# Dealing score units later and more evenly, and moving every second turned tile's copy to VectorE

## The chip, the cores and the metric

The kernel runs on one core of a Trainium2 chip. A core has TensorE (matmuls; PE in the profile, its weight loads PEld), VectorE (DVE), ScalarE (ACT), GpSimd (POOL) and SyncE (SP, which here only issues DMAs). The metric is the device time of one launch in microseconds, the median of the runs.

## The reference

Two transformer layers over x (4 batches, 512 tokens, 320 features), with a context of 1601 rows of 192 features per batch. Each layer is self attention, cross attention to the context and a gated feed forward, each behind a layer norm and with a residual:

```python
h1 = _ln(x, n1_g, n1_b)
x = _attn(h1, h1, q1, k1, v1, o1_w, o1_b, heads) + x          # 20 heads of 16
h2 = _ln(x, n2_g, n2_b)
x = _attn(h2, context, q2, k2, v2, o2_w, o2_b, heads) + x
h3 = _ln(x, n3_g, n3_b)
a, g = jnp.split(h3 @ ff_w1 + ff_b1, 2, axis=-1)
x = a * jax.nn.gelu(g, approximate=False) @ ff_w2 + ff_b2 + x
```

Attention is the exact softmax: the maximum of each row of scores is taken off before the exponential.

## The kernel before

**Groups, steps and beats.** A layer of a batch is a block; there are 8 blocks (i = 0 to 7). Attention is done in groups of 4 heads: 5 groups for each block's self attention (kind S, 4 tiles of 128 keys) and 5 for its cross attention (kind C, 13 tiles). One tile of keys of one group is a step; there are 680 steps. Ten phases (PHASES) interleave the cross attention of block c with the self attention of block c+2. Each step has four beats. At beats 0 and 2 TensorE makes scores of two heads each (`scores`, line 1303) into two banks `pr`, and ScalarE takes their exponentials (line 1020). At beat 3 TensorE multiplies the exponentials of the step before with the values (`weigh`, line 1320).

**Fills.** All other matmul work (projections, transposes, feed forward) is cut into fills, mostly one per odd beat, which share one bank `pf`. TensorE may begin a fill only when the one before it has been copied out (`fill_free`). The fills of this change are the transposes: `t1`, `t2` (layer norm output turned, 3 per block, copied with gain and bias into `hT` by ScalarE, line 964) and `tc` (context turned, 8 per block, copied into `cT` by ScalarE, lines 1007 and 1008; the fourth and eighth hold only 65 columns, with one column more copied by an instruction of its own). `v1`, `k2`, `q2`, `ff2` are projections.

**Units.** Before a group's scores can be made, the row maxima must be known. They come from units: a matmul pair into one of two banks `pd` (line 1287), and a maximum over its columns on VectorE (line 1111). An S group has 8 units of 2 x 512 columns, a C group 32 units of 2 x 400 (or 402) columns. When all are done VectorE forms the negated maxima (lines 1123 to 1135), and GpSimd issues a DMA that puts them into rows of the queries QS (`put_maxima`, line 913); the group's first scores wait for that (`max_in`). A unit needs its group's queries and keys in SBUF: SyncE stages them from DRAM scratch (`stage_group`, lines 781 and 786), at beats in STAGE_AT.

**The planner.** Which beat makes which units is worked out in plain Python ahead of the kernel. `beat_times` gives each beat a planned time AT, in its own microseconds. A group's units may be dealt from UNITS_FROM, which is AT at the staging beat plus STAGED_IN (6.0 for S, 8.0 for C), and should be dealt by UNITS_TO, 9.5 before the group's first step. At each even beat (in a step with one short fill: at beat 0 alone, with two places) the planner works out a rate, what is left over the time left, and a need, what is left over the places left, rounded up. The credit grows by rate x time, is at least the need, and is capped at the need or 2; whole credits are dealt as units, to the group of lowest number first:

```python
        _need = max(_need, -(-_sum * unit_places(_b) // _count))
    _credit = min(max(_credit + _rate * (_next - _now), _need), max(_need, MOST_UNITS))
    while _credit >= 1.0:
```

All engines run their lists of instructions in order of beats. At a beat VectorE does the work beside (norm statistics, residual adds, gates), then the reductions of that beat's units, then reciprocals. `set_key_rows` (lines 1044 to 1050, four memsets of KS) stands behind the work of the first beat (-1), ahead of the first units.

Of the kernel before, what the change touches and what calls it, by code (L numbers as in the profile page):

```python
# [12 lines left out]
P = 128  # L13
# [355 lines left out]


AT = beat_times()
STAGED_IN = {"S": 6.0, "C": 8.0}
LAST_UNIT_AHEAD, PUT_BEHIND, MOST_UNITS = 9.5, 0.5, 2

BEATS_AHEAD, LEAST_BEATS = 6, 8
# [22 lines left out]
for _q in GROUPS:  # L398
    for _part in range(-1, len(HALVES[_q.kind])):
        _stored = BEAT_OF[split_for(_q, _part)]  # L400
        _at = max(4 * read_until(_q, _part) if read_until(_q, _part) else FIRST_BEAT,
                  _stored + STORE + STAGE_BEHIND if _stored >= 0 else FIRST_BEAT)
        STAGE_AT.setdefault(_at, []).append((_q, _part))

        UNITS_FROM[_q.n, _part] = max(AT[_at] + STAGED_IN[_q.kind] if _at >= 0 else 0.0, UNITS_FROM.get((_q.n, -1), 0.0))
    UNITS_TO[_q.n] = AT[4 * _q.step0] - LAST_UNIT_AHEAD


# [11 lines left out]
for _b in range(0, BEATS, 2):  # L420
    if not unit_places(_b):
        continue
    _now = AT[_b]
    _next = AT[min(_b + 2 * unit_places(_b), BEATS - 1)]

    _rate, _need, _sum = 0.0, 0, 0
    for _n in sorted(n for n in _left if _left[n]):
        if units_now(_n, _now):
            _first_beat.setdefault(_n, _b)
        if _n not in _first_beat:  # L430
            continue
        _sum += units_now(_n, _now)
        _rate = max(_rate, _sum / max(UNITS_TO[_n] - _now, 0.5))
        _last = max(4 * GROUPS[_n].step0 - BEATS_AHEAD, min(_first_beat[_n] + LEAST_BEATS, 4 * GROUPS[_n].step0))
        _count = sum(unit_places(b) for b in range(_b, max(_last, _b + 2)))
        _need = max(_need, -(-_sum * unit_places(_b) // _count))
    _credit = min(max(_credit + _rate * (_next - _now), _need), max(_need, MOST_UNITS))
    while _credit >= 1.0:
        _n = next((n for n in sorted(_left) if _left[n] and units_now(n, _now)), None)
        if _n is None:  # L440
            break
        UNITS_AT[_b].append((_n, len(GROUPS[_n].units) - _left[_n]))
        _left[_n] -= 1
        _credit -= 1.0
        if not _left[_n]:
            assert _b < 4 * GROUPS[_n].step0
            PUT_AT.setdefault(min(beat_at(_now + PUT_BEHIND), 4 * GROUPS[_n].step0 - 1), []).append(GROUPS[_n])
# [33 lines left out]

def fills_at(beat):
    return sum(p[0] in STAGE for p in PLACES.get(beat, []))


LATE = {b for b in PLACES if 0 <= b < BEATS and b % 4 == 1 and fills_at(b) < 2 and not fills_at(b + 2)}
# [8 lines left out]
def blocks_kernel(nc, x, ctx_in, w, out):  # L495
    es = ExitStack()
    with es:
# [436 lines left out]
        def _(act):  # L934
# [8 lines left out]
            def beside(stage, i, f):  # L943
# [5 lines left out]
                if stage == "w" and f:  # L949
# [2 lines left out]
                    act.wait_ge(fill_ready, FILLS_BEFORE[stage, i, f])  # L952
                    hold(j)
                    copy(high_tile(j, P, KC * P), raw[:, :, :].rearrange("p k n -> p (k n)")).then_inc(raw_high, 1)
                if stage not in STAGE or stage in ("o1", "o2", "a", "ff2"):
                    return
                no = FILL[stage, i, f]
                pf, done = bank(no), free(no)
# [81 lines left out]
        def _(dve):  # L1040
            v = nc.vector
            dve.wait_ge(consts, CONSTS)
            v.tensor_copy(identr[:, :], DEN["S"][:, 0:P]).then_inc(identr_set, 1)
            def set_key_rows():

# [31 lines left out]
            def beside(stage, i, f):  # L1077
                l, b = i // B, i % B
                if stage in LN_STAGES:
                    measure(stage, i, f)  # L1080
                if stage == "n3" and i == N - 1:
                    if f:
                        normalise_last(f - 1)
                    if f == TT - 1:
                        normalise_last(f)
                if stage == "t3" and i == N - 1:
                    m = DC[f][1]
                    dve.wait_ge(h_high, KC * i + f + 1)
                    v.tensor_tensor(HS[0:m, 1, f, :], hT[0:m, f, :], HS[0:m, 0, f, :].bitcast(F32), ALU.subtract
                                    ).then_inc(h_low, 1)  # L1090
                if stage in ("o1", "o2", "ff2"):
                    s, no = {"o1": "n1", "o2": "n2", "ff2": "n3"}[stage], FILL[stage, i, f]
                    dve.wait_ge(bias_done, TT * LN0[s, i] + f + 1)
                    dve.wait_ge(fill_ready, no + 1)
                    v.tensor_tensor(X[:, b, f, :], bank(no)[:, 0:D], X[:, b, f, :], ALU.add).then_inc(free(no), 1)  # L1095
                if stage == "a":
                    no, side = FILL[stage, i, f], uT[:, f * T:(f + 1) * T]
                    if i < N - 1:
                        dve.wait_ge(gelu_done, FM * i + f + 1)
                    else:  # L1100
                        own, count = freed_through(FILL["g", i, f])[-1]
                        dve.wait_ge(own, count)
                    dve.wait_ge(fill_ready, no + 1)
                    v.scalar_tensor_tensor(side, bank(no)[:, :], b1col[:, l, 0, f:f + 1], side, ALU.add, ALU.mult
                                           ).then_inc(free(no), 1)
# [279 lines left out]
```

## Time and profile before

| | |
|---|---|
| median of 3 runs | 3407.88 us (3406.81 to 3412.51) |
| the profiled execution's own time | 3404.07 us |
| its span | 3402.3 us |
| PE, DVE, ACT, POOL busy | 3070.3 (90%), 2051.4 (60%), 1896.9 (56%), 729.4 us (21%) |
| units: reductions on VectorE | 1600, 1599.3 us in all |
| exponentials on ScalarE | 2720, 1478.4 us in all |
| mean granted TensorE clock | 0.96 |

The span is one execution from first to last instruction. A wait is put down to the instruction or DMA that ended it; "issue" stands where the profile shows no releaser. PEclk is the granted clock as a share of 2.4 GHz: 0.50 is the level of 1.2 GHz.

### The profile page before, as it was taken

The page shows a single profiled execution, that of the slowest core. Times are in us where ns is not written, and L with a number is a line of the kernel's source. Part 1 is how long each engine was busy: PE and PEld are TensorE (multiplying, and loading weights), DVE is VectorE, ACT ScalarE, POOL GpSimd, SP SyncE. Part 2 cuts the span into 40 slices and gives each one's busy share as a digit, 9 for nine tenths or more (in the row PEclk, how much of TensorE's full clock was granted, in tenths as well). Part 3 has the DMA queues.
Part 4 walks back from the last instruction along what each step waited for, and adds up shares of the span by engine and source line. Part 5 has one row for each costly group of instructions (what it writes and reads, how often), then busy time and mean ns, then how long its engine had stood idle before and what let it go on. Part 6 is the DMA issues. An engine that isn't in the chain of part 4 may idle for free.

```text
span 3402.3 us, 43794 instructions
## 1 busy us (share of the span) xinstructions
PE 3070.3 (90%) x16000; PEld 1412.6 (42%) x16000; DVE 2051.4 (60%) x2732; ACT 1896.9 (56%) x3646; POOL 729.4 (21%) x972
## 2 busy tenths in 40 slices
PE   4987888899999999999999899999998999998998
PEld 1332333334354343544345343453434543543445
DVE  5655655666656666656765576566665576666521
ACT  1643555656664566645665566745666466646631
POOL 2342221312302132022320223121231004002000
PEclk8997979999999999999999999999999999999999
DMA  6543334433433435433333334333243214322212
GB/s 158 154 111 93 112 85 120 126 110 84 129 105 83 129 81 148 108 90 117 98 117 88 118 94 136 100 96 104 64 125 101 79 40 137 96 51 49 73 38 78
DMA packets 208597, 342.27 MB, mean 101 GB/s; under 512 B 25464, under 2 KB 107776, under 8 KB 207104
## 3 DMA queue, kind: packets, MB, share of 16 engines
q1 hardware_dynamic: 203264, 338.09, 36.0%
q8 instruction: 128, 2.10, 0.3%
q0 software_dynamic: 5120, 1.39, 0.2%
q14 instruction: 85, 0.70, 0.1%
HBM read 202.29 MB, written 114.75 MB: 93 GB/s over the span
## 4 chain that ended last, share of the span: by engine, by line
PE 64%; DVE 14%; DMA 8%; ACT 6%; issue 4%; POOL 3%; SPq 2%; DVEq 0%; ACTq 0%; POOLq 0%
PE pr L1303 14%; PE po L1320 12%; DVE mx L1111 10%; PE pd L1287 7%; PE pf L1170 5%; PE pf L1223 5%; PE pf L1236 5%; ACT ET L1020 3%; PE pf L1193 3%; PE pf L1211 3%; DMA QS<-scr_q 3%; PE pf L1202 3%; DVE DEN L1119 2%; PE pf L1228 2%; DMA WS<-parts 1%
## 5 line engine op out<-in xcount | busy, mean ns | idle before, releaser
L1020 ACT ACTIVATE ET<-pr 128x512 f32<-128x512 f32 (+1 forms) x2720 | 1478.4, 597 | 1311.8 <-PE pr L1303 1300.0
L1111 DVE TENSOR_REDUCE mx<-pd 128x2 f32<-128x800 f32 (+2 forms) x1600 | 1599.3, 1031 | 941.9 <-PE pd L1287 939.3
L1303 PE MATMUL pr<-QS,KS 64*128 64x512 f32 (+1 forms) x2720 | 851.9, 503 | 70.6 <-ACT ET L1020 48.1
L1287 PE MATMUL pd<-KS,QS 64*128 64x400 f32 (+2 forms) x3200 | 633.7, 378 | 164.3 <-DVE mx L1111 102.1
L1320 PE MATMUL po<-ET,V 128*32 128x512 f32 (+2 forms) x5440 | 750.2, 625 | 0.5 <-ACT OU L1026 0.5
L1303 PEld LDWEIGHTS pr<-QS,KS 64*128 64x128 f32 (+1 forms) x2720 | 339.6, 185 | 907.4 <-ACT ET L1020 649.5
L1287 PEld LDWEIGHTS pd<-KS,QS 64*128 64x128 f32 x3200 | 373.2, 193 | 259.6 <-DVE mx L1111 167.2
L896 POOL TENSOR_TENSOR HS<-uT,HS 128x512 fp32r<-128x512 f32 (+4 forms) x168 | 190.1, 1132 | 613.0 <-ACT uT L984 612.7
L913 POOL DMA_DIRECT2D QS<-MT x160 | 94.1, 590 | 937.2 <-DVE MT L1135 934.5
L1223 PE MATMUL pf<-HS,WS 128*128 128x512 f32 x665 | 191.3, 418 | 13.1 <-issue 10.6
L1320 PEld LDWEIGHTS po<-ET,V 128*32 128x32 f32 (+2 forms) x5440 | 107.1, 108 | 208.2 <-issue 197.0
L1119 DVE RECIPROCAL DEN<-DEN 128x128 f32<-128x128 f32 (+1 forms) x192 | 168.9, 918 | 20.4 <-DMA OA<-OU 19.7
L1193 PE MATMUL pf<-cT,w_kv 96*128 96x400 f32 (+3 forms) x384 | 160.8, 542 | 9.3 <-ACT uT L984 5.3
L1236 PE MATMUL pf<-w_a,uT 128*128 128x320 f32 x560 | 158.1, 437 | 0.0
L921 POOL TENSOR_TENSOR OA<-OA,DEN 128x128 f32<-128x128 f32 (+1 forms) x192 | 84.9, 454 | 326.0 <-DVE DEN L1119 325.6
L1170 PE MATMUL pf<-hT,w_a 128*128 128x512 f32 (+1 forms) x288 | 139.7, 622 | 9.4 <-ACT uT L984 7.7
L1095 DVE TENSOR_TENSOR X<-pf,X 128x320 f32<-128x320 f32 x89 | 43.7, 491 | 171.2 <-PE pf L1236 119.4
L1223 PEld LDWEIGHTS pf<-HS,WS 128*128 128x128 f32 x665 | 115.7, 190 | 70.0 <-issue 34.1
L1202 PE MATMUL pf<-w_kv,cT 96*128 96x128 f32 (+3 forms) x832 | 139.6, 315 | 0.9 <-ACT V L988 0.5
L881 POOL TENSOR_SCALAR uT<-X,mv,rstd 128x320 f32<-128x320 f32 x92 | 133.9, 1456 | 9.7
L1211 PE MATMUL pf<-wo,OA 128*128 128x320 f32 x366 | 128.9, 473 | 4.7 <-POOL OA L921 3.5
L1202 PEld LDWEIGHTS pf<-w_kv,cT 96*128 96x128 f32 (+1 forms) x832 | 115.3, 189 | 29.2 <-issue 13.0
(81 smaller groups left out, 2053.2 us busy)
## 6 DMA issues: line engine op xcount, KB each, us to landing
WS<-parts SPq DMA_DIRECT2D x160, 320.0 KB, 3.0
QS<-scr_q SPq DMA_DIRECT2D x80, 512.0 KB, 5.8
scr_k<-HS SPq DMA_DIRECT2D x144, 200.0 KB
scr_q<-HS SPq DMA_DIRECT2D x96, 256.0 KB
KS<-scr_k SPq DMA_DIRECT2D x80, 300.8 KB, 5.2
KS<-scr_k SPq DMA_DIRECT2D x80, 300.0 KB, 6.1
KS<-scr_k SPq DMA_DIRECT2D x80, 192.0 KB, 4.8
scr_k<-HS SPq DMA_DIRECT2D x48, 256.0 KB
```

Of the source, the lines that this page charges most:

```text
L1020: activation(ET[0:q.rows[k], s % 2, 2 * pair + e, :], pr[e][0:q.rows[k], :], ACT.Exp).then_inc(score_free, 1)
L1111: v.reduce_max(mx[q.kind][:, t, 2 * p:2 * p + 2, c], pd[no % 2][:, :, 0:cols], AX_X).then_inc(unit_free, 1)
L1119: v.reciprocal(own, own).then_inc(inverted, 1)
L1170: ins = mm(pf[0:m, :], wsq[stage][:, k, r:r + m], hT[:, k, :], start=k == 0, stop=k == KC - 1)
L1193: ins = mm(pf[0:m, 0:cols], w_kv2[:, 0, k, r:r + m], cT[:, k, n0:n0 + cols], start=k == 0, stop=k == 1)
L1202: ins = mm(pf[0:m, to:to + (h1 - h0) * DH], cT[:, k, j * P:j * P + m], w_kv2[:, 1, k, h0 * DH:h1 * DH], start=k == 0, stop=k == 1)
L1211: ins = mm(pf[:, 0:D], OA[kind][0:m, k, t * P:(t + 1) * P], wo[0:m, which, k, :], start=k == 0, stop=k == KC - 1)
L1223: mm(pf[:, :], W[:, s, :], HS[:, 0, k, :], start=s == 0, stop=False)
L1236: ins = mm(pf[:, 0:D], uT[:, m * T + t * P:m * T + (t + 1) * P], wff2[:, m, :], start=m == 0, stop=m == FM - 1)
L1287: ins = mm(pd[no % 2][:, e, 0:cols], queries[:, t * P:(t + 1) * P], keys, start=True, stop=True)
L1303: mm(pr[e][0:m, :], keys, queries, start=True, stop=True).then_inc(score_ready, 1)
L1320: ins = mm(po[32 * h:32 * h + own.shape[1], :], own, ET[0:m, s % 2, h, :], start=k == 0, stop=k == q.kt - 1)
```

## The change

Four edits. First, units: S and C groups alike may be dealt units from 10.0 planned microseconds behind their staging (before: 6.0 and 8.0), and from 7.0 for the first ten groups, which run without a cross attention beside them (before: 6.0). Second, the need is kept as a fraction instead of being rounded up. Third, of the fills `t1`, `t2` and `tc` those with an odd f are copied out by VectorE: one of three for `t1` and `t2`, four of eight for `tc`. Fourth, since VectorE now reads the gains `gcol`, it waits at its start for the small loads (`small_in`), which ScalarE did already.

```diff
-STAGED_IN = {"S": 6.0, "C": 8.0}
+STAGED_IN, STAGED_ALONE = 10.0, 7.0
...
-        UNITS_FROM[_q.n, _part] = max(AT[_at] + STAGED_IN[_q.kind] if _at >= 0 else 0.0, UNITS_FROM.get((_q.n, -1), 0.0))
+        UNITS_FROM[_q.n, _part] = max(AT[_at] + (STAGED_ALONE if _q.n < 2 * G else STAGED_IN) if _at >= 0 else 0.0, UNITS_FROM.get((_q.n, -1), 0.0))
...
-    _rate, _need, _sum = 0.0, 0, 0
+    _rate, _need, _sum = 0.0, 0.0, 0
...
-        _need = max(_need, -(-_sum * unit_places(_b) // _count))
+        _need = max(_need, _sum * unit_places(_b) / _count)
...
-    while _credit >= 1.0:
+    while _credit >= 0.999:
...
+def taken_by_vector(stage, f):
+
+    return stage in ("t1", "t2", "tc") and f % 2 == 1
...
-                if stage not in STAGE or stage in ("o1", "o2", "a", "ff2"):
+                if stage not in STAGE or stage in ("o1", "o2", "a", "ff2") or taken_by_vector(stage, f):
                     return
...
             dve.wait_ge(consts, CONSTS)
+            dve.wait_ge(small_in, 16 * 2 * L)
...
+                if stage in ("t1", "t2", "tc") and taken_by_vector(stage, f):
+                    no = FILL[stage, i, f]
+                    dve.wait_ge(fill_ready, no + 1)
+                    if stage == "tc":
+                        c, (k0, k1) = f // len(TC_CHUNKS), TC_CHUNKS[f % len(TC_CHUNKS)]
+                        n0, cols = k0 * P, min(J, k1 * P) - k0 * P
+                        if k1 == JT:
+                            v.tensor_copy(cT[:, c, J:JP], bank(no)[0:CC, cols - 1:cols])
+                        v.tensor_copy(cT[:, c, n0:n0 + cols], bank(no)[0:CC, 0:cols]).then_inc(free(no), 1)
+                    else:
+                        s, m = int(stage[1]) - 1, DC[f][1]
+                        if LOWS_BEFORE[stage, i, f]:
+                            dve.wait_ge(h_low, LOWS_BEFORE[stage, i, f])
+                        v.tensor_scalar(hT[0:m, f, :], bank(no)[0:m, :], gcol[0:m, l, s, 0, f:f + 1],
+                                        gcol[0:m, l, s, 1, f:f + 1], ALU.mult, ALU.add).then_inc(free(no), 1)
```

## Rows read from the trace of the kernel before

**Rows 1.** The page's head and busy line: busy us, share of the span, instructions.

```profile
span 3402.3 us, 43794 instructions
PE 3070.3 (90%) x16000; PEld 1412.6 (42%) x16000; DVE 2051.4 (60%) x2732; ACT 1896.9 (56%) x3646; POOL 729.4 (21%) x972
```

**Rows 2.** Waits, whole span: engine, line waited for: us in total, times, longest.

```profile
PE pd L1287 <- DVE mx L1111: 102.1, 159, 2.7
...
PE pd L1287 <- issue: 53.9, 13, 16.6
...
PE pr L1303 <- ACT ET L1020: 48.1, 83, 6.3
...
PE pr L1303 <- DMA QS<-MT: 21.6, 7, 6.1
```

**Rows 3.** Groups of instructions by shape: S units' matmuls; busy, mean ns, idle before.

```profile
L1287 PE MATMUL pd<-KS,QS 64*128 64x512 f32 x640 | 140.5, 454 | 92.4 <-issue 53.9 <-DVE mx L1111 31.4 <-DMA QS<-scr_q 5.5
```

**Rows 4.** Timeline of PE, 1282 to 1295 us: start, us, what, [idle before].

```profile
1281.40 0.56 PE L1303 MATMUL pr<-QS,KS 64*128 64x512 f32 x2
...
1285.41 0.55 PE L1303 MATMUL pr<-QS,KS 64*128 64x512 f32 x2
1290.02 1.22 PE L1287 MATMUL pd<-KS,QS 64*128 64x512 f32 x4 [4.05 <-issue]
1291.17 3.03 PE L1193 MATMUL pf<-cT,w_kv 96*128 96x400 f32 x4
```

**Rows 5.** Windows of 8 us behind S groups' first units: window, us, busy times, PEclk, DMA.

```profile
343.90:351.90 8.00, 7.43 (x28) 3.57 (x28) 7.02 (x8) 2.25 (x5) 1.80 (x4) 0.67 0.14 39
...
1290.00:1298.00 8.00, 7.98 (x24) 3.15 (x26) 4.71 (x4) 1.88 (x4) 1.03 (x1) 0.50 0.51 165
...
2560.80:2568.80 8.00, 7.95 (x48) 3.85 (x48) 5.81 (x5) 2.43 (x5) 0.00 (x0) 0.79 0.36 98
```

**Rows 6.** The chain that ended last, 1275 to 1300 us: start, us, what.

```profile
1281.04 7.94 DMA QS<-scr_q
```

**Rows 7.** Timeline of PE, then of DVE, 1448 to 1465 us.

```profile
1453.05 0.49 PE L1287 MATMUL pd<-KS,QS 64*128 64x512 f32 x2 [0.58 <-DVE mx L1111]
...
1450.64 4.62 DVE L1111 TENSOR_REDUCE mx<-pd 128x2 f32<-128x1024 f32 x4
```

**Rows 8.** Waits of 186 to 328.7 us alone.

```profile
PE pd L1287 <- DVE mx L1111: 12.8, 22, 0.9
```

**Rows 9.** Groups by shape: reductions of C and S units, ScalarE's two copies.

```profile
L1111 DVE TENSOR_REDUCE mx<-pd 128x2 f32<-128x800 f32 x960 | 918.5, 985 | 537.1 <-PE pd L1287 536.3
L1111 DVE TENSOR_REDUCE mx<-pd 128x2 f32<-128x1024 f32 x320 | 373.8, 1216 | 203.3 <-PE pd L1287 202.1
...
L964 ACT ACTIVATE hT<-pf,gcol 128x512 f32<-128x512 f32 x47 | 36.8, 782 | 29.2 <-PE pf L1163 29.2
...
L1008 ACT COPY cT<-pf 96x512 f32<-96x512 f32 x48 | 28.0, 584 | 1.2 <-PE pf L1184 1.2
```

**Rows 10.** Timeline of DVE in a step with a turned context tile.

```profile
1243.55 1.89 DVE L1111 TENSOR_REDUCE mx<-pd 128x2 f32<-128x800 f32 x2 [1.15 <-PE pd L1287]
```

**Rows 11.** Start of the span: timeline; landing time of the loads of line 819.

```profile
3.95 0.43 SPq L819 DMA_DIRECT2D b1col<-ff_b_dram  x1
...
8.23 0.23 DVE L1043 CAST identr<-DEN 128x128 fp32r<-128x128 f32 x1 [8.23 <-POOL V L867]
...
12.35 6.25 DVE L1047 MEMSET KS<- 16x7432 f32 x1 [1.48 <-issue]
...
22.70 0.78 ACT L964 ACTIVATE hT<-pf,gcol 128x512 f32<-128x512 f32 x1 [1.21 <-PE pf L1163]
...
60.56 1.22 PE L1287 MATMUL pd<-KS,QS 64*128 64x512 f32 x4 [16.59 <-issue]
...
DMA to landing us min/median/max: 5.9/6.1/6.2
```

**Rows 12.** Timeline of PE, 2463 to 2476 us: a group's first scores.

```profile
2473.84 0.80 PE L1303 MATMUL pr<-QS,KS 64*128 64x512 f32 x2 [3.93 <-DMA QS<-MT]
```

## The prediction

> **What bounds the kernel now.** I read the page's head first: TensorE is busy for 3070.3 of 3402.3 us, VectorE for 60% and ScalarE for 56% [rows 1]. So the time is TensorE's: its work, plus what it idles, 332 us, plus what it loses while its clock is low. Next the list of waits, to see what ends TensorE's idle time. The largest entry is units: 102.1 us in 159 waits for a reduction that has not yet emptied a bank, and 53.9 us in 13 waits with no releaser named [rows 2]. The groups by shape say which units those 13 are: all are S units of 512 columns, which have 5.5 us more put down to the DMA of the queries [rows 3]. One of the 13 is the first unit of the kernel, 16.59 us [rows 11]. That leaves 53.9 - 16.6 = 37.3 us in 12 waits, and 5.5 us: 42.8 us of idle time in which TensorE stands at the first unit of an S group.
>
> The timeline shows one: scores at 1285.41, then nothing until 1290.02 [rows 4]. The chain gives the releaser that the wait does not: the DMA of that group's queries, issued at 1281.04, 7.94 us long [rows 6]. So the unit stands in TensorE's list before its data can be there; with "issue" the reader is to see a DMA. No C group's first unit waits: the shapes of 400 and 402 columns have nothing but reductions before them.
>
> Then the windows. Behind the wait TensorE is busy for 7.98 of 8 us, but at a granted clock of 0.50, the level of 1.2 GHz [rows 5]; a `k2` fill of four matmuls takes 3.03 us there [rows 4]. I took such a window behind the first unit of 13 S groups that had waited. Their clocks run from 0.50 to 1.00, and 8 x (1 - clock) adds up to 25.8 us (first, worst and last are in [rows 5]). Each long wait is paid for nearly twice.
>
> The waits for reductions are of another kind. Two S units in each of two successive even beats give VectorE four reductions, 4.62 us in a row, while TensorE goes through the short half of a step in less than half of that; the fourth unit waits 0.58 us [rows 7]. Such a burst comes out of rounding up: with 31 units left for 28 places the need is 2, not 1.1, so the planner deals two per beat until it is ahead, then one, and later none.
>
> **The change part by part.** The sum is made against the profiled execution, 3404.07 us, of which 1.8 us lie outside the span; the median is 3.8 us above it, which I add at the end.
>
> *S groups from 10.0 instead of 6.0.* For the group of the example the planner's times are: staged at 979.5, first unit at 987.1. From 989.5 on, the first even beat is the one at 990.9, two even beats (one step) later. TensorE takes 4.0 us for a step here (1281.40 to 1285.41, [rows 4]), and the wait was 4.05 us, so even this one ends about when the keys land. Other waits are 2 to 3 us and go; two early ones, of 7.65 and 4.61 us, may leave a remnant. Meanwhile C units are at hand to fill the beats. I take 4 us as left: **-39 us** (between -30 and -42.8). S maxima are not pressed: this group's first step is planned at 1028.4, 49 planned us behind its staging. With the long waits goes the low clock behind them, nine tenths of 25.8: **-23 us** (between -13 and -26).
>
> *C groups from 10.0 instead of 8.0.* There is no wait to remove. It costs places: each C group begins one even beat later, so that more units share the rest. The price is inside the next term.
>
> *Fractional needs.* Of the 102.1 us, 12.8 lie between 186 and 329 us [rows 8], where 40 units must pass in ten even beats, three to six per beat or pair of them; rounding does not matter there, and the C group starts a beat later: nothing gained. Of the other 89.3 us the runs of double S units and the doubles of C units go, since the rate then deals by planned time: two in the long halves of steps, one in the short ones. What stays are waits behind a group's maxima (some 1.5 us of small VectorE work), and the stretch of `t2` and `tc` steps. I worked the planner through there: 31 units for 25 places from its first S unit on, two places per step; the credit is capped at the need of 2.5, two are dealt, the need creeps up to 3, and the last four steps get three units each. VectorE then has 3 x 0.985 us [rows 9] plus a copy of some 0.7 us, in a step that lasts 3.04 us with two units (1.89 busy, 1.15 idle, [rows 10]) and a little more with three. I take 44% of the 89.3 us as removed, since I can follow the bursts away and not these: **-39 us** (between a fifth, -17, and two thirds, -61).
>
> *The last units come later.* Rounding up had units dealt ahead of their due time; now the last goes out one even beat later in some C groups. Behind it are the maxima, GpSimd's DMA and the first scores. One such wait exists: 3.93 us at 2473.84, where the transfer landed late [rows 12]; there are only seven in all, 21.6 us [rows 2], so most groups have room for one beat. **+8 us**, one more of that kind with its low clock (between 0 and +40).
>
> *Copies moved to VectorE.* Of 48, 32 have 512 columns: 16 from `hT`'s line, 0.782 us on ScalarE, and 16 from `cT`'s, 0.584 us [rows 9]. Nothing in the trace is such a copy on VectorE. The two reductions from PSUM give a slope: (1216 - 985) / 224 = 1.03 ns per column and 160 ns fixed, so 512 columns take 0.69 us, an estimate. With the 16 small pairs (65 columns and one, by the same line 0.23 + 0.16 us) that is 28.5 us more on VectorE. In a step with a context tile VectorE waits 1.15 us for its next unit [rows 10], so the copy fits where two units are dealt. The cover is gone where three are: +1 us taken, and all 28.5 us as the upper bound. VectorE's order puts nothing new in front of anybody: the fill is ahead of the next units on TensorE as well. On ScalarE the gain is bounded by TensorE's waits for exponentials in these steps, 0.1 to 0.5 us each within the 48.1 us of [rows 2]: **-3 us** (0 to -7).
>
> The Trainium skill speaks against this part: "VectorE: DVE Perf Modes", in its section on the TRN2 errata, has a PSUM source cost 120 cycles plus the columns at 0.96 GHz on VectorE, 172 plus the columns at 1.2 GHz on ScalarE. By that the copy would be an estimated 0.66 us on VectorE against 0.57 us on ScalarE, so the move makes the work itself longer; 28.5 us would become some 27. By the same formula the reduction of 1024 columns is 1.19 us, and the trace has 1.216 us.
>
> *The start.* VectorE begins at 8.23 us; the last small load is issued at 3.95 and takes at most 6.2 us, so it begins by 10.2 us [rows 11], and the first norm behind it. **+1.6 us** (0 to +1.9). Also the copy of `t1`'s second tile now stands before the four memsets of KS, the first of which began at 12.35 us; four of 6.25 us with three gaps of about 1.5 us take 29.5 us. That tile's copy began on ScalarE at 22.70 us [rows 11]; with 1.6 us of delay, 0.7 us of copy and 1.5 us of gap the memsets run from about 26.5 to 56 us. The first unit starts at 60.56 [rows 11], 4 us later, so this is hidden; without that cover each microsecond would count in full.
>
> The sum: -39 - 23 - 39 + 8 + 1 - 3 + 1.6 = -93.4; 3404.1 - 93.4 = 3310.7, and with 3.8 us to the median 3314 us.
>
> **The rivals.**
> *Only the DMA part holds.* The bursts form again, against the due times instead of ahead of them, and the copies sit in VectorE's full steps. For it: the 10.0 for C groups gives up places, and the hand-worked stretch ends in steps of three. Against: VectorE has 40% idle. Then -62 + 1.6 + 8 + 14 (half of the copies' time) = -38, 3369 us.
> *Slower: late maxima.* If the last units slip by two even beats, first scores wait as at 2473.84: 3.9 us, and about 4 us more of low clock behind it, 8 us per group. It decides from twelve groups on (93 / 8); in half of the 40 C groups it would be +160 us, 3474 us. For it: needs no longer force units forward. Against: UNITS_TO still stands 9.5 planned us ahead and the rate grows without bound as it nears, so that two beats are hard to lose.
> *No change.* The S transfer is released by the scores of an earlier step; should it be late for the queue and not for its issue, the units would wait at their new place. Then -15 for clock and bursts and +15 for the copies: 3408 us. Against: the queries of the example had landed at 1289 us [rows 6], whenever the unit is dealt.
> *More than forecast.* All of the 42.8, 25.8 and 89.3 us go, and 3 us of ScalarE, at no cost: 3247 us.
>
> **How the numbers follow.** The forecast gets 0.58, with its own range of 3280 to 3345; only the DMA part 0.24; late maxima 0.06; no change 0.05; more than forecast 0.07. The range goes from 3272, which takes about half of the last case, to 3375, just past the second: all but about 0.15 is inside. Faster by over 0.2% (what a measurement of this kernel can tell): 0.58 + 0.24 + 0.07 and 0.01 of no change, 0.90. Within 0.2%: 0.03. Slower: 0.06 and 0.01, 0.07.
>
> **What would show it.** In the waits, the 12 of TensorE for units without a releaser are down to two or three, and PEclk stays at 1.00 behind S groups' first units. The wait of `pd` for `mx` falls from 102.1 to about 60 us, and what is left stands in steps with three units. VectorE shows 32 copies of 0.6 to 0.75 us. QS<-MT grows by less than 10 us. The prediction is wrong if QS<-MT is ended by dozens of waits, if the keys' landing moves with the units, or if the first unit starts more than 2 us later than 60.56.

## The result and the profile after

| | before | after |
|---|---|---|
| median of 5 runs each, us | 3406.81 (3400.98 to 3412.51) | 3369.36 (3357.46 to 3381.6) |
| ratio, 95% interval | | 0.9896 (0.9865 to 0.9927) |
| profiled execution, us | 3404.07 | 3375.84 |
| its span; mean granted clock | 3402.3; 0.960 | 3374.0; 0.955 |

The change makes the kernel 1.04% faster, 37 us, where 93 were forecast. The time is inside the range (3272 to 3375), but by its upper end, where the rival "only the DMA part holds" had put it (3369 us).

The page's head of the kernel after, to hold against [rows 1]:

```profile
span 3374.0 us, 43804 instructions
PE 3074.7 (91%) x16000; PEld 1422.6 (42%) x16000; DVE 2072.7 (61%) x2796; ACT 1877.2 (56%) x3582; POOL 729.1 (22%) x972
```

The span of the profiled execution is 28.3 us shorter (the medians are 37.5 apart; the profiled execution of after lies 6.5 us above its median): TensorE idles 32.7 us less (332.0 to 299.3) and is busy 4.4 us more, for the same 16000 matmuls. I had forecast that busy time would fall, by the 23 us of low clock.

Waits of TensorE after, whole span (engine, line waited for, us in total, times, longest), against [rows 2]:

```profile
PE pd L1308 <- DVE mx L1132: 89.9, 135, 2.2
PE pr L1324 <- DMA QS<-MT: 51.2, 15, 6.8
PE pr L1324 <- ACT ET L1025: 44.7, 76, 4.9
...
PE pd L1308 <- DMA KS<-scr_k: 13.2, 1, 13.2
...
PE pd L1308 <- issue: 3.8, 1, 3.8
```

Units without their data: 59.4 us are now 17.0, of which 13.2 are the kernel's first unit. Units behind reductions: 102.1 to 89.9. First scores behind the maxima's DMA: 21.6 in 7 waits to 51.2 in 15. The last takes back 29.6 us of idle time; what that was worth in time is asked in the fourth series.

Groups by shape (busy, mean ns, idle before), S units' matmuls against [rows 3], then VectorE's new copies:

```profile
L1308 PE MATMUL pd<-KS,QS 64*128 64x512 f32 x640 | 137.4, 429 | 38.3 <-DVE mx L1132 21.1 <-DMA KS<-scr_k 13.2 <-issue 3.8
...
L1110 DVE TENSOR_SCALAR hT<-pf,gcol 128x512 f32<-128x512 f32 x16 | 12.9, 805 | 12.0 <-PE pf L1184 11.8
L1105 DVE COPY cT<-pf 96x512 f32<-96x512 f32 x16 | 10.8, 672 | 8.8 <-PE pf L1205 8.8
L1105 DVE COPY cT<-pf 96x65 f32<-96x65 f32 x16 | 3.4, 212 | 0.0
```

Windows of 8 us after (busy times, granted clock, DMA share, GB/s). The first begins with the late first scores of a C group, the second with the first unit of the S group that [rows 4, 5] show waiting:

```profile
878.30:886.30 8.00, 7.98 (x26) 3.32 (x26) 3.57 (x4) 3.10 (x7) 0.82 (x1) 0.50 0.75 191
1285.30:1293.30 8.00, 7.66 (x42) 2.99 (x41) 3.69 (x4) 5.53 (x12) 2.06 (x2) 1.00 0.42 117
```

Behind that S unit the clock is at 2.4 GHz where it was at 1.2. The level of 1.2 GHz now stands behind a wait of another kind.

The start after, timeline of VectorE and TensorE, against [rows 11]:

```profile
10.22 0.23 DVE L1049 CAST identr<-DEN 128x128 fp32r<-128x128 f32 x1 [10.22 <-DMA b1col<-ff_b_dram]
...
24.70 0.81 DVE L1110 TENSOR_SCALAR hT<-pf,gcol 128x512 f32<-128x512 f32 x1 [11.85 <-PE pf L1184]
...
50.55 6.25 DVE L1056 MEMSET KS<- 2x7432 f32 x1 [1.60 <-issue]
...
59.52 1.22 PE L1308 MATMUL pd<-KS,QS 64*128 64x512 f32 x4 [13.20 <-DMA KS<-scr_k]
```

The first unit is a microsecond earlier than before, not later.

### The profile page after: what moved, and what is told of

Its sections match the earlier page's. It is cut to its first block, busy times and chain, and to the rows that moved or that the text cites. A ratio compares the mean times of both kernels' runs of the same rounds, so it can differ in the third digit from the quotient of the medians.

```text
span 3374.0 us, 43804 instructions
## 1 busy us (share of the span) xinstructions
PE 3074.7 (91%) x16000; PEld 1422.6 (42%) x16000; DVE 2072.7 (61%) x2796; ACT 1877.2 (56%) x3582; POOL 729.1 (22%) x972
## 4 chain that ended last, share of the span: by engine, by line
PE 67%; DVE 13%; DMA 6%; ACT 6%; POOL 4%; issue 3%; SPq 2%; DVEq 0%; ACTq 0%; POOLq 0%
PE pr L1324 15%; PE po L1341 14%; DVE mx L1132 8%; PE pd L1308 7%; PE pf L1191 5%; PE pf L1244 5%; PE pf L1257 4%; PE pf L1214 4%; PE pf L1232 3%; ACT ET L1025 3%; PE pf L1223 3%; DVE DEN L1140 3%; DMA QS<-MT 2%; PE pf L1249 2%; DMA WS<-parts 1%
## 5 line engine op out<-in xcount | busy, mean ns | idle before, releaser
L1324 PE MATMUL pr<-QS,KS 64*128 64x512 f32 (+1 forms) x2720 | 860.9, 506 | 96.6 <-DMA QS<-MT 51.2
L1308 PE MATMUL pd<-KS,QS 64*128 64x400 f32 (+2 forms) x3200 | 620.3, 376 | 107.3 <-DVE mx L1132 89.9
```

The source lines that it names most:

```text
L1308: ins = mm(pd[no % 2][:, e, 0:cols], queries[:, t * P:(t + 1) * P], keys, start=True, stop=True)
L1324: mm(pr[e][0:m, :], keys, queries, start=True, stop=True).then_inc(score_ready, 1)
```

## The experiments

There are fifteen, in four series; each kernel's ratio is to the kernel before, run beside it on the same chip. A "step of three" below is one of the steps that have both of their places for units at beat 0 (at most one short fill beside them) and are dealt three units or more there. They are counted in the planner's lists, which it makes before anything runs: 46 in the kernel before, 47 in the kernel after.

| kernel | us | ratio (95%) | pd for a reduction | QS<-MT | low clock |
|---|---|---|---|---|---|
| before | 3401 to 3407 | 1 | 102.1 | 21.6 | 273 |
| after | 3369.36 | 0.9896 (0.9865-0.9927) | 89.9 | 51.2 | 300 |
| staging alone | 3427.28 | 1.0068 (1.0051-1.0086) | 143.7 | 21.5 | 257 |
| fractions alone | 3412.67 | 1.0023 (1.0012-1.0033) | 96.3 | 56.1 | 340 |
| copies alone | 3405.76 | 0.9992 (0.9976-1.0008) | 108.9 | 19.1 | 273 |
| all but copies | 3369.16 | 0.9897 (0.9881-0.9914) | 87.5 | 61.5 | 287 |
| after, C 8.0 | 3361.5 | 0.9884 (0.9863-0.9905) | 90.7 | 50.2 | 267 |
| staging of S alone | 3384.41 | 0.9945 (0.9924-0.9966) | 119.5 | 21.1 | 246 |
| after, 10 beats ahead | 3396.35 | 0.998 (0.9967-0.9993) | 122.5 | 20.7 | 269 |
| after, due 14 ahead | 3390.46 | 0.9953 (0.9935-0.9972) | 109.1 | 27.7 | 313 |
| after, halved reductions | 3269.11 | 0.961 (0.9583-0.9637) | 31.6 | 46.5 | 202 |
| before, halved reductions | 3290.98 | 0.9666 (0.9639-0.9693) | 33.2 | 17.4 | 212 |
| after, C 7.0 | 3352.59 | 0.9854 (0.983-0.9877) | 79.1 | 44.2 | 273 |
| after, C 7.0, MOST 2.5 | 3344.36 | 0.983 (0.9805-0.9854) | 80.5 | 38.8 | 263 |
| after, maxima put first | 3352.01 | 0.985 (0.9827-0.9874) | 91.4 | 16.4 | 253 |
| the last two together | 3338.47 | 0.9803 (0.9778-0.9828) | 74.5 | 14.5 | 245 |
| before, maxima put first | 3389.48 | 0.9954 (0.9937-0.9971) | 102.4 | 10.0 | 236 |

The last three columns are of each profiled execution, in us: two entries of the chain of waits, and the time in which the records show a granted clock under full.

### First series: the parts, one by one

**Staging alone.** The new times with the needs rounded up as before, and ScalarE's copies.

```diff
-STAGED_IN = {"S": 6.0, "C": 8.0}
+STAGED_IN, STAGED_ALONE = {"S": 10.0, "C": 10.0}, 7.0
...
```

> The kernel before with the staging times alone (10.0, and 7.0 for the first ten groups); needs are still rounded up and ScalarE copies all tiles. Theory A (fractions cost): the 42.8 us of waits at S groups' first units go and part of the low clock behind them, the last units stay where they were (12 even-and-odd beats ahead for 29 of 40 C groups), so QS<-MT stays near its 22 us and the time falls by 45 to 65 us, below the changed kernel. Theory B (the 10.0 of C groups costs): late maxima show up here already, QS<-MT near 50 us, and the time falls by 35 us or less.

It is 0.68% slower, and the theory by which the later times alone bring most of the gain falls. The S units' waits go (20.0 us named "issue" are left, 15.7 of them the first unit), but the waits for reductions rise by 41.6 us: rounded needs pack the units that begin later into what places are left (the planner's steps of three rise from 46 to 61). The waits of the kernel "staging alone":

```profile
PE pd L1287 <- DVE mx L1111: 143.7, 212, 3.0
...
PE pr L1303 <- DMA QS<-MT: 21.5, 6, 6.2
PE pd L1287 <- issue: 20.0, 4, 15.7
```

**Fractions alone.**

```diff
-    _rate, _need, _sum = 0.0, 0, 0
+    _rate, _need, _sum = 0.0, 0.0, 0
...
-        _need = max(_need, -(-_sum * unit_places(_b) // _count))
+        _need = max(_need, _sum * unit_places(_b) / _count)
...
-    while _credit >= 1.0:
+    while _credit >= 0.999:
```

> The kernel before with fractional needs alone. Theory A: the last unit of 15 of the 40 C groups moves from 12 or 10 beats to 8 beats ahead of the first scores, QS<-MT grows from 22 to about 50 us with low clock behind it, the waits for reductions fall by at most 15 us, and the time rises by 10 to 30 us. Theory B: fractions are worth the 15 us of waits that they remove, QS<-MT stays near 22 us, and the time falls by 10 to 20 us. My forecast had it at -31 us.

Slower as well, by 0.23%: 5.8 us less behind reductions, but 34.5 us more behind the maxima's DMA, and 66 us more at a low clock.

**Copies alone**, with VectorE's wait for the small loads.

```diff
+                if stage in ("t1", "t2", "tc") and taken_by_vector(stage, f):
+                    ...
+                    v.tensor_scalar(hT[0:m, f, :], bank(no)[0:m, :], ...)
```

> The kernel before with VectorE's copies of every second turned tile and its wait for the small loads, nothing else. Theory A: within 5 us of before, since VectorE has the room where two units are dealt. Theory C (the copies are what ate the gain): 32 copies of 0.67 to 0.8 us push reductions back in the t2 and tc steps, the waits of pd for mx grow by 10 us or more and the time rises by 10 to 20 us.

**All but the copies.** The kernel after, with `taken_by_vector` false throughout and without VectorE's wait for the small loads.

> The changed kernel with ScalarE copying all tiles again and without VectorE's wait for the small loads; staging times and fractional needs as changed. Theory A: within 5 us of the changed kernel (3369). Theory C: 10 to 20 us faster than it, near 3352.

Both answer alike: the copies do nothing that can be measured, alone (0.9992) or in company (3369.16 against 3369.36 us). What is left is an interaction: two edits that cost 0.68% and 0.23% each gain 1.03% together. The table shows where. Fractions add about as much behind the maxima's DMA in either company (34.5 us to the kernel before, 40.0 us to "staging alone"), but they take 5.8 us off the waits for reductions in the first and 56.2 us in the second (143.7 to 87.5). So the later times add waits for reductions, and the fractions take them off again.

### Second series: where the dealing gives back

**C's time back at 8.0**, in the kernel after.

```diff
-STAGED_IN, STAGED_ALONE = 10.0, 7.0
+STAGED_IN, STAGED_ALONE = {"S": 10.0, "C": 8.0}, 7.0
...
```

> The changed kernel with C groups dealt from 8.0 again (S groups from 10.0, fractional needs and copies as changed). Theory D (later staging takes places away, and that is what packs units): steps with three or more units at two places fall from 47 to 41, waits of pd for mx fall by 5 to 15 us and the time by 5 to 15 us against the changed kernel (3369). Theory E (late maxima and the low clock behind them are what ate the gain, the C time is neutral): last units stay where they are, QS<-MT stays near 51 us, and the time is within 5 us of 3369.

The median is 8 us lower, as theory D has it, but the waits for reductions do not fall (90.7 us) and QS<-MT stays at 50.2, as theory E has it; 8 us is less than the intervals. Neither theory is decided by this run.

**Only the S units' time**, in the kernel before: 10.0 and 7.0 for S, 8.0 for C, needs rounded.

> The kernel before with S groups from 10.0 (7.0 for the first ten groups) and nothing else: C groups from 8.0, needs rounded up, ScalarE's copies. With both times at 10.0 and rounded needs it was 3427 us, with 143.7 us of waits of pd for mx. Theory D: much of those 39 us more came from the C time; here the waits are near 115 us and the time is at or below before (3404), down to 3385. Theory F (the S time itself turns its wait into bursts as long as needs are rounded up, since the same units come in fewer beats): waits near 140 us and a time of 3415 to 3430.

With rounded needs, C at 10.0 instead of 8.0 is the difference between 0.9945 and 1.0068, 43 us; with fractions, between 0.9884 and 0.9896, less than the intervals. S alone gives 20 us, with 119.5 us of waits for reductions, near what theory D gave; theory F falls. A wait that was short before grows in it, here 4 us long, in the timeline of TensorE:

```profile
1277.99 0.74 PE L1287 MATMUL pd<-KS,QS 64*128 64x512 f32 x4 [0.58 <-issue]
1282.69 3.03 PE L1193 MATMUL pf<-cT,w_kv 96*128 96x400 f32 x4 [3.96 <-ACT uT L984]
```

The keys' fill `k2` waits for ScalarE, which itself stands 4.88 us for a tile of the ring to be stored. Such waits come to 19.3 us, where they were 5.3 in the kernel before: TensorE, no longer held up by S units, runs into the next queue. ScalarE's timeline of that kernel has the other end of it:

```profile
1281.74 0.50 ACT L981 ACTIVATE HS<-pf 128x400 fp32r<-128x400 f32 x1 [4.88 <-DMA scr_q<-HS]
```

**Units ten beats ahead of need**, **and due 14.0 instead of 9.5 planned us ahead**, both in the kernel after.

```diff
-BEATS_AHEAD, LEAST_BEATS = 6, 8
+BEATS_AHEAD, LEAST_BEATS = 10, 8
```

```diff
-LAST_UNIT_AHEAD, PUT_BEHIND, MOST_UNITS = 9.5, 0.5, 2
+LAST_UNIT_AHEAD, PUT_BEHIND, MOST_UNITS = 14.0, 0.5, 2
```

> The changed kernel with BEATS_AHEAD 10 in place of 6: needs have all units dealt ten beats ahead of the first scores, so the last unit of every C group goes out 12 beats ahead (in the changed kernel: 15 groups at 8, 12 at 10, 13 at 12). The steps with three or more units rise from 47 to 80. Theory E: QS<-MT falls from 51 to about 22 us and low clock with it, and the time falls by 15 to 35 us even if waits for reductions grow by 10 to 20 us. Theory D: what is taken off QS<-MT comes back in waits for reductions, time within 10 us of 3369 or above.

> The changed kernel with LAST_UNIT_AHEAD 14.0 in place of 9.5: the rate aims 4.5 planned us earlier. Last units at 8 beats fall from 15 to 8 groups, 22 groups are at 14 or 16; steps with three or more units fall from 47 to 33, beats with two in one place rise from 334 to 396. Theory E: QS<-MT falls to 30 to 40 us and the time by 10 to 20 us. Theory D or F: doubles make more waits for reductions, 100 us or more, and the time does not fall.

The late maxima go as wished (20.7 and 27.7 us), and both kernels are slower than the kernel after: the waits for reductions come to 122.5 and 109.1 us. In the first the steps of three rise from 47 to 80. In the second they fall to 33, but beats with two units in one place rise from 334 to 396, so that steps of three alone do not tell the waits. With this falls the theory that the late maxima are what to take away from the dealing: bought by dealing, earlier maxima cost more than they bring.

### Third series: what the reductions are worth, and C's time

**Halved reductions**, in the kernel after and in the kernel before. The maxima are taken over half of the columns, so part of the computation is left out; TensorE's work and the dealing stay.

```diff
-                v.reduce_max(mx[q.kind][:, t, 2 * p:2 * p + 2, c], pd[no % 2][:, :, 0:cols], AX_X).then_inc(unit_free, 1)
+                v.reduce_max(mx[q.kind][:, t, 2 * p:2 * p + 2, c], pd[no % 2][:, :, 0:cols // 2], AX_X).then_inc(unit_free, 1)
```

> The kernel after with each reduction reading only the first half of its unit's columns, so the maxima are taken over half of the columns (the output changes). The dealing of units and all of TensorE's work stay. Theory T (after the change a good part of the time still lies in TensorE waiting for a reduction to give a buffer back, some 90 us by its chain of waits, and in the low clock that these bring): reductions of about 600 ns for 985 and 1216 ns take most of it away, the time falls by 70 to 110 us, to 3260 to 3300 us, and the wait of matmuls for a reduction falls below 30 us. The waits for the late maxima (51 us of QS<-MT) stay above 35 us if they are late because their last unit is dealt late, and fall below 25 us if VectorE's backlog makes them late. Rival (TensorE is bound by its own 3075 us and by other waits that take the place of these): a fall of less than 40 us, with QS<-MT or waits for DMAs up by as much as the reductions' wait goes down.

> The kernel before with the same halved reductions (maxima over half of the columns; the output changes). It shows what is left of the change once reductions never hold a matmul up. If the change gained by spacing units (needs as fractions), its gain is now less than before: the ratio of the halved kernel after to this one lies between 0.990 and 1.000, and this one falls by 90 to 130 us from 3404, to 3275 to 3315 us. If the change gained by the units of S alone (waits for their staging DMA, 39 us, which no reduction touches), this kernel stays 30 to 45 us behind the halved kernel after.

The groups by shape and two waits of the halved kernel after:

```profile
L1132 DVE TENSOR_REDUCE mx<-pd 128x2 f32<-128x400 f32 x960 | 520.5, 570 | 676.4 <-PE pd L1308 672.8
```

```profile
PE pr L1324 <- DMA QS<-MT: 46.5, 15, 5.3
PE pd L1308 <- DVE mx L1132: 31.6, 64, 1.6
```

A reduction takes 570 ns instead of 985; 58 us of waits go and 100 us of time, since TensorE's busy time also falls, by 44.0 us (3074.7 to 3030.7) with 98 us less at a low clock, and its idle time by 63.0 us in all. So each microsecond of these waits is paid 1.7 times here, and 1.6 times in the kernel before (68.9 us of waits, 110 us of time). QS<-MT hardly moves (51.2 to 46.5): VectorE's backlog does not make the maxima late. The halved kernels stand 22 us apart, a ratio of 0.993. That is inside what was expected if the change gained in part by spacing the units, and outside the 30 to 45 us of the S waits alone. In idle time TensorE has 24.9 us less in the halved kernel after (42.5 us less at units without their data, the kernel's first included, 29.1 us more behind maxima, the rest in small waits), and its busy time is 1.6 us longer.

**C's time at 7.0**, without and with MOST_UNITS at 2.5. The line of MOST_UNITS is changed in the second kernel alone.

```diff
-STAGED_IN, STAGED_ALONE = 10.0, 7.0
-LAST_UNIT_AHEAD, PUT_BEHIND, MOST_UNITS = 9.5, 0.5, 2
+STAGED_IN, STAGED_ALONE = {"S": 10.0, "C": 7.0}, 7.0
+LAST_UNIT_AHEAD, PUT_BEHIND, MOST_UNITS = 9.5, 0.5, 2.5
...
```

> The kernel after with C's time at 7.0 alone: steps with three units or more 34 (47 after, 41 at 8.0), last units as after (14, 13 and 13 groups at 8, 10 and 12 beats ahead). Theory T (a third unit in a short step costs about 1.2 us wherever it stands, and the late maxima stay as they are): 7 to 13 steps less by 1.2 us each, 3352 to 3366 us, with QS<-MT still 45 to 55 us. Rival (C's time does nothing with needs as fractions): 3366 to 3373 us, equal to the kernel after.

> The kernel after with C's time at 7.0 instead of 10.0 and MOST_UNITS 2.5 instead of 2: steps with three units or more are 27 (47 after), last units of C stand 8, 10, 12 and 14 beats ahead for 9, 10, 20 and 1 of 40 groups (15, 12 and 13 after). Theory T (late maxima and packed units are two prices of one dealing): the wait for late maxima falls from 51 to 30 to 40 us and the steps of three units from about 70 to about 40 us of excess; the time is 3345 to 3362 us, ratio 0.982 to 0.988. Rival (what is won in one comes back in the other, as in the two kernels with later or earlier last units): pd's wait for a reduction rises from 90 to over 105 us and the time stays at 3362 to 3380 us.

At 7.0 the kernel is at 0.9854 instead of 0.9896; against "all but copies", the same kernel within 0.2 us and with the narrower interval, the intervals are just apart (0.983 to 0.9877 and 0.9881 to 0.9914); against the kernel after's own, wider one (0.9865 to 0.9927) they overlap. Steps of three fall from 47 to 34, the waits for reductions by 10.8 us. The rival (nothing comes of it) falls by the first comparison, narrowly: 10.0 for C costs 0.4% against 7.0. Against the 8.0 of the kernel before it is not shown to cost anything, as the second series has it. MOST_UNITS at 2.5 brings the median down by another 8 us, but the intervals overlap and the profiled executions stand 0.5 us apart, so that it is not shown to be a gain.

### Fourth series: the maxima's DMA in GpSimd's list

In the kernel after twelve groups' first scores wait over 1 us for the maxima, four before. For ten of the twelve VectorE has the maxima ready 2.4 to 10.1 us before GpSimd issues their DMA. One of them in the timelines of VectorE, GpSimd and TensorE of the kernel after:

```profile
867.04 0.89 DVE L1156 STREAM_TRANSPOSE MT<-MS 32x32 f32<-32x32 f32 x4
```

```profile
870.19 1.26 POOL L901 TENSOR_TENSOR HS<-uT,HS 128x512 fp32r<-128x512 f32 x1 [1.22 <-ACT uT L989]
871.40 1.22 POOL L918 DMA_DIRECT2D QS<-MT  x2
```

```profile
878.32 0.80 PE L1324 MATMUL pr<-QS,KS 64*128 64x512 f32 x2 [3.94 <-DMA QS<-MT]
```

Ready at 867.93, issued at 871.40. In between GpSimd ends the low part of one query tile, waits 1.22 us for ScalarE's half of the next, and takes 1.26 us for its low part: both are ahead of the DMA in its list. The edit, in the kernel after, in the kernel with C 7.0 and MOST_UNITS 2.5, and in the kernel before:

```diff
             for beat in range(FIRST_BEAT, BEATS + BEATS_BEHIND + 1):
+                for q in PUT_AT.get(beat, []):
+                    put_maxima(q)
                 for p in PLACES.get(beat, []):
                     beside(*p)
                 if beat == FIRST_BEAT:
                     put_maxima(GROUPS[0])
-                for q in PUT_AT.get(beat, []):
-                    put_maxima(q)
```

> The kernel after with one edit: in GpSimd's list the DMA that puts a group's maxima into the queries stands ahead of the low parts of that beat's tiles instead of behind them. In the kernel after, twelve groups' first scores wait over 1 us for this DMA, and for ten of them VectorE has the maxima ready 2.4 to 10.1 us before GpSimd issues it (one, of 3.94 us: ready at 867.9, a tile's low part from 870.2, issued at 871.5). Theory G (the maxima come late through GpSimd's order, not through the dealing): the waits of the ten, 38 us in all, go but for small remnants, and QS<-MT falls from 51.2 to 10 to 22 us; with the low clock behind them, 15 to 35 us more, the time is 3305 to 3340 us, ratio 0.970 to 0.981. Theory D (they are late because the last unit is dealt late): QS<-MT stays above 40 us and the time at 3360 to 3372 us. Rival (the low parts, now later, are waited for by the stores and by the ring of tiles): QS<-MT falls, but ScalarE's wait for a free ring tile rises and the time stays over 3350 us.

> The kernel after with C's time at 7.0, MOST_UNITS 2.5 and the maxima's DMA ahead of the low parts. Without the last edit it had 38.8 us of waits for that DMA, nine of eleven groups of the same kind. Theory G: QS<-MT 10 to 20 us, and 25 to 45 us faster than without the edit: 3300 to 3322 us, ratio 0.969 to 0.976. Theory D: no change, 3340 to 3350 us.

> The kernel before with the maxima's DMA ahead of the low parts. It has four such waits over 1 us, and only two of them with the maxima ready long before the issue (10.5 us at a wait of 4.5, 6.7 us at one of 6.1). Theory G: at most 10 us of waits to be had, and 23 groups in which the order delays the DMA without anybody waiting; the time falls by 3 to 18 us, ratio 0.995 to 0.999, so that against this kernel the whole change would be worth more than 1.04%: 2 to 3%, near its forecast. Theory D: 0.999 to 1.001.

The same place in the kernel "maxima put first", GpSimd's timeline, and its waits:

```profile
853.59 1.22 POOL L918 DMA_DIRECT2D QS<-MT  x2 [1.33 <-DVE MT L1156]
854.87 1.26 POOL L901 TENSOR_TENSOR HS<-uT,HS 128x512 fp32r<-128x512 f32 x1
```

```profile
PE pr L1324 <- DMA QS<-MT: 16.4, 9, 6.0
PE pf L1214 <- ACT uT L989: 15.4, 16, 3.0
```

GpSimd now waits for VectorE alone, and that group's first scores wait 0.52 us. QS<-MT falls from 51.2 to 16.4 us, as theory G has it and against theory D: most of the waits named so need GpSimd's order, and the dealing used up the slack that had hidden it. The times missed their range, though: 3352 and 3338 us where 3305 to 3340 and 3300 to 3322 were expected. The rival comes out by its own numbers: the low parts are later now, ScalarE's waits for the ring's stores rise from 6.5 to 20.5 us, `k2`'s wait for ScalarE rises from 4.5 to 15.4 us, and the time stays over 3350. The kernel before gains 0.46% too, 14 us by medians for 11.6 us less behind this DMA: its low clock falls from 273 to 236 us. So against that kernel the change is worth 0.985 / 0.9954 = 0.9895, what it was worth at the outset, and my 2 to 3% on that footing was wrong. The order explains where the 29.6 us stood, not why the change brought 37 us instead of 93.

By its interval the kernel after with this edit (0.9827 to 0.9874) is apart from "all but copies" (0.9881 to 0.9914), but not from the kernel after itself (0.9865 to 0.9927). The kernel with all three edits has the lowest time of those that compute everything, 3338.47 us, ratio 0.9803 (0.9778 to 0.9828): 31 us under the kernel after, apart from it and from the kernel before.

## Why the prediction was wrong, by its steps

The sign was right, the size was not: 37 us came of 93. Two steps failed most, each by 27 us. The low clock was priced as a pure gain of 23 us, and TensorE's busy time rose by 4.4; and the waits for reductions were to fall by 39 us and fell by 12.2. The term for late maxima was mis-sized by 21.6 us of waits. Behind the last two stands one mistake: edits of one planner were costed as if they added up.

- **S groups from 10.0, -39: right.** 59.4 us of such waits became 17.0; the kernel's first unit takes 3.4 of that, so 39.0 us went. The remnant is one wait of 3.8 us, the early one named.
- **The low clock, -23: right where I looked, wrong in the sum.** Taking 8 x (1 - clock) behind the same 13 units, 25.8 us became 4.0. But over the whole span that sum rose, from 137 to 150 us, and TensorE's busy time by 4.4: some 35 us of it stand elsewhere now. Of 42 stretches at 1.2 GHz (38 before), sorted by the wait that took most of the time just ahead of each, about 18 follow waits for reductions (10 before), 15 waits of scores (9 before) and 2 late data of units (12 before); how far ahead one looks moves these counts by a few. I had priced the clock behind the waits that go, and but for one late group's 4 us behind none that stay, move or come. The step is off by 27 us.
- **Fractional needs, -39: mis-sized, 12.2 us measured.** Steps with two units at each of two beats went where I had followed them (32 to 8 in steps 125 to 465), but only in part over the whole list (68 to 32), and steps of three did not go (46 to 47). They only moved: in one stretch from four `t2` and `tc` steps to the last five `tc` steps behind. A step with three units takes 4.4 us there (842.20 to 846.58), as three-unit steps did in the kernel before; two-unit steps took 3.0 to 3.2 us. VectorE's timeline of the kernel after shows it:

```profile
842.20 2.79 DVE L1132 TENSOR_REDUCE mx<-pd 128x2 f32<-128x800 f32 x3 [1.01 <-PE pd L1308]
...
846.58 2.79 DVE L1132 TENSOR_REDUCE mx<-pd 128x2 f32<-128x800 f32 x3 [0.98 <-PE pd L1308]
849.28 0.68 DVE L1105 COPY cT<-pf 96x512 f32<-96x512 f32 x1
850.92 2.79 DVE L1132 TENSOR_REDUCE mx<-pd 128x2 f32<-128x800 f32 x3 [0.96 <-PE pd L1308]
```

  I had worked such a stretch through, seen it end in threes, and still given the average 44%. And the 12.2 us are a net: the later times by themselves add 41.6 us of these waits (17.4 of them with S alone later), and the fractions take 56.2 off the same kernel ("staging alone" to "all but copies"). I had given the later times no price here. In time C's 10.0 costs 7.9 us against the 8.0 of before by medians, less than the intervals, and 17 us against 7.0.
- **Last units later, +8: mis-sized, 29.6 us measured.** Eight more waits instead of one. "Some C groups" were 25 of 40 by the planner's lists, 21 by one even beat and 4 by two; fifteen now have their last unit 8 beats ahead of their scores (two before), and all nine C groups that wait over 1 us are of these. The room that I had read out of "most groups don't wait" was partly spent already in GpSimd's list: 23 groups of the kernel before have their maxima lie ready for over 1 us. In time this step explains little: with the DMA put first in both kernels the change is worth the same 0.9895.
- **Copies, +1, and ScalarE, -3: near nothing, as priced; their signs can't be told.** VectorE's copies take 29.3 us in all where 28.5 were forecast, and show in no time. Waits for exponentials fell from 48.1 to 44.7, but "all but copies" has 45.2: most of that is not the copies' doing. The plain copy of 512 columns takes 0.672 us, by the estimate of 0.69; the one with gain and bias takes 0.805. The Trainium skill's formula ("VectorE: DVE Perf Modes", the section on the TRN2 errata) gives an estimated 0.66 us: the trace agrees for the plain copy, and has 0.15 us more for the one with two operands per partition. The total by this formula, which the prediction puts at some 27 us, is 26.
- **The start, +1.6: hidden.** VectorE begins at 10.22 us and the last memset ends at 56.80, as worked out; the first unit starts at 59.52, and is put down to the keys' DMA.

By name the idle time is: S units -39.0, first unit -3.4, reductions -12.2, maxima +29.6, exponentials -3.4, all else -4.3, together -32.7; with +4.4 busy, -28.3. Forecast minus measured, in waits: 26.8 for reductions, 21.6 for maxima; in busy time, 27.4. These 75.8 us, less some 11 us by which the start and the small waits did better, are the distance between the forecast -93.4 and -28.3. ("All else" holds one more late S unit of the kernel before, 1.2 us for its keys, which the 42.8 us leave out.)

Of the rivals, "only the DMA part holds" gave 3369 us, and 3369.36 was measured. That is luck in good part. Its reason was partly right: the bursts do form again against the due times. But its 14 us for copies in VectorE's full steps did not come, its 23 us of clock were not gained over the span, and the late maxima were 29.6 us where it has 8. "Slower: late maxima" had its mechanism right and its size wrong: twelve long waits (four before), not twenty, and of them only nine in C groups.

What stays open: why the first scores of group 0 wait 5 to 6 us in every kernel, and those of one late C group (block 7, the third of its five) in all but two (0.96 us in the halved kernel after, none in "before, maxima put first"); and why the dealing of the kernel after brings more low clock than that of the kernel before. Neither was tried apart.

## What to carry to other kernels

When a planner's rule is changed, price the stalls by re-counting its whole list (how many steps hold three or four units, how far ahead each last unit is), not by the one burst that is seen to go: units that leave one place stand in another. Put a price on the clock behind every wait that stays or comes, not only behind those that go: here a microsecond of waits for reductions was worth 1.7. And before a data transfer is called late because its work was dealt late, look at when its input was ready and what stands ahead of its issue on the issuing engine; here the DMA stood 3.5 us behind 1.2 us of another engine's delay and 2.3 us of GpSimd's own work.

## What was not expected of the hardware

How much clock a wait costs was not fixed by its length. Of the 13 late S units of the kernel before, one that had waited 2.84 us was followed by 8 us at the full clock, one of 2.39 us by 8 us in which 8 x (1 - clock) is 3.4 us, and the longest, 7.65 us, by 2.7 us. The kind of wait did not fix it either: the granted clock stood at 0.50 over 8 us behind a late unit in the kernel before and over 8 us behind late maxima in the kernel after, with TensorE busy for 7.98 us of both. Over the kernels run the time at a low clock went from 202 to 340 us. "Fractions alone", with 34.5 us less of waits for S units and reductions than the kernel before and 34.5 us more for maxima, idles 11 us less in all, and still had 66 us more of low clock and 20.6 us more of busy time (3090.9). So where the waits stand weighed more than their sum; what it is about the place was not tried apart.
